# A linear recurrence layer on one core: x tiles spread unevenly over the level steps, tables requested sooner, narrower matmuls in the early levels of half 2

## The reference

```
h  = layernorm(x) * (1 + ca) + sa                # ca, sa, ga, ... from silu(c) @ wmod
per channel d:  s_t = A[d] s_{t-1} + Bm[d] h_t   # 16x16 matrix A[d], 8192 steps
                y_t = Cm[d] . s_t + Dm[d] h_t
x  = x + ga * (h + gelu(layernorm(y)*w + b) @ W_out.T + b_out)
h  = layernorm(x) * (1 + cb) + sb
x  = x + gb * (per-feature relu net of (h @ Win) @ Wout + bout)
```

## Time and profile before

| | |
|---|---|
| runs shown | 767.56, 768.90, 769.18 us; median 768.9 |
| profiled execution | 774.0 us; span of the core in it 772.2 us; mean granted TensorE clock 0.984 |
| PE busy | 710.3 us, 92% |
| DVE, POOL, ACT busy | 534.2, 483.1, 470.9 us (69, 63, 61%) |
| level steps of half 1 | 10.5 to 113 us |
| level steps of half 2 | 216.6 to about 276 us |
| output stage | 389 us to the end |

### The profile page before, as it was taken

One profiled execution on the slowest core, in us unless ns is written; L12 is line 12 of the kernel. 1 busy time (PEld: TensorE's weight loads), 2 busy tenths in 40 slices (PEclk: granted clock), 3 DMA queues, 4 the chain that ended last, 5 costly groups with the idle time before them and its releaser, 6 DMA issues.

```text
span 772.2 us, 24718 instructions
## 1 busy us (share of the span) xinstructions
PE 710.3 (92%) x10079; PEld 496.8 (64%) x10079; DVE 534.2 (69%) x1192; ACT 470.9 (61%) x1007; POOL 483.1 (63%) x684
## 2 busy tenths in 40 slices
PE   5777979899999988898879999999999999999997
PEld 4656667788799977887634555554555555455564
DVE  7765867854653367745734688888888788887776
ACT  1647677133322363234345788888888888888872
POOL 5654561753445615763188987789888888887710
PEclk9989999999999999999979999999999999999999
DMA  7967500139600000289342003322322332231114
GB/s 216 324 234 250 204 3 17 43 78 176 161 7 5 4 17 10 57 197 201 93 183 110 1 1 110 106 88 81 110 83 83 111 109 83 83 109 55 47 45 156
DMA packets 78257, 78.18 MB, mean 101 GB/s; under 512 B 16192, under 2 KB 49600, under 8 KB 78144
## 3 DMA queue, kind: packets, MB, share of 16 engines
q1 hardware_dynamic: 77120, 74.76, 31.9%
q10 hardware_dynamic: 1024, 1.84, 0.9%
HBM read 59.28 MB, written 17.30 MB: 99 GB/s over the span
## 4 chain that ended last, share of the span: by engine, by line
PE 49%; DVE 1%; POOL 0%; ACT 0%; DVEq 0%; issue 0%; ACTq 0%; POOLq 0%
PE PS L1304 30%; PE PS L1373 4%; PE PS L1351 4%; PE PS L1296 4%; PE PS L1338 4%; PE PS L1388 1%; PE PS L1314 1%; PE PS L1325 0%; ACT arenaC L660 0%; DVE ebs L975 0%; PE PS L1318 0%; DVE arenaC L991 0%; DVEq L81 0%; POOL sy L388 0%; DVE XY L829 0%
## 5 line engine op out<-in xcount | busy, mean ns | idle before, releaser
L1304 PE MATMUL PS<-arenaC,arenaA 128*128 128x512 f32 x512 | 242.2, 606 | 0.0
L404 POOL TENSOR_TENSOR arenaC<-arenaA,par 128x512 f32<-128x512 f32 x104 | 107.2, 1039 | 86.1 <-ACT arenaA L643 41.6
L1304 PEld LDWEIGHTS PS<-arenaC,arenaA 128*128 128x128 f32 x512 | 90.2, 191 | 87.8 <-issue 83.3
L1167 PE MATMUL PS<-arenaA,arenaC 64*64 64x80 f32 x1792 | 121.4, 236 | 18.6 <-DVE arenaC L817 13.5
L1170 PE MATMUL PS<-arenaA,arenaC 64*64 64x64 f32 x1792 | 118.7, 221 | 1.6 <-issue 1.6
L696 ACT ACTIVATE arenaA<-PS,ffc 128x256 f32<-128x256 f32 x224 | 111.7, 577 | 12.3 <-PE PS L1351 12.3
L1167 PEld LDWEIGHTS PS<-arenaA,arenaC 64*64 64x64 f32 x1792 | 94.1, 139 | 26.0 <-DVE arenaC L817 15.6
L1021 DVE SCALAR_TENSOR_TENSOR PS<-arenaA,ffc,PS 128x256 f32<-128x256 f32 x196 | 95.2, 486 | 22.3 <-ACT arenaA L696 5.7
L817 DVE STREAM_TRANSPOSE arenaC<-arenaC 128x512 f32<-128x512 f32 x104 | 72.6, 703 | 42.2 <-POOL arenaC L404 38.4
L1170 PEld LDWEIGHTS PS<-arenaA,arenaC 64*64 64x64 f32 x1792 | 98.6, 137 | 1.8 <-issue 1.8
L668 ACT ACTIVATE arenaA<-PS,lnwb 128x256 f32<-128x256 f32 x128 | 65.7, 574 | 44.5 <-PE PS L1296 44.5
(11 more groups left out here) (198 smaller groups left out, 1251.9 us busy)
## 6 DMA issues: line engine op xcount, KB each, us to landing
arenaC<-kernel_taps SPq DMA_DIRECT2D x64, 256.0 KB, 4.6
XY<-in_L_attn_x SPq DMA_DIRECT2D x38, 256.0 KB, 6.1
arenaC<-in_L_attn_x SPq DMA_DIRECT2D x15, 512.0 KB, 3.7
out<-arenaC SPq DMA_DIRECT2D x15, 512.0 KB, 2.7
arenaC<-in_L_attn_x SPq DMA_DIRECT2D x26, 256.0 KB, 4.8
XY<-in_L_wmod SPq DMA_DIRECT2D x6, 1024.0 KB, 9.0
XY<-in_L_attn_x SPq DMA_DIRECT2D x11, 512.0 KB, 3.6
out<-XY SPq DMA_DIRECT2D x10, 512.0 KB, 2.8
```

Source lines behind the costliest of these rows:

```text
L404: gp.tensor_tensor(BDs[:, step % BDR, :, :].rearrange("p g (a m) -> p g a m", m=NS), src, msk, ALU.mult).then_inc(S["bdp_r"], 1)
L1167: pe.matmul(pv_ps(r)[e:e + BW, j, 0:LW + NS], BDTs[e:e + BW, b, j, :], PV[e:e + BW, g, PW - LW:PW + NS], start=True, stop=True)
L1304: mm = pe.matmul(PS[:, 2 + t, :], zT[:, u % 2, q, t * P:(t + 1) * P], WoT[:, q, :], start=False, stop=(q == QB - 1))
```

## The change

Five edits: (1) `stats_of` and `tiles_of` follow two tables. The statistics are 2 tiles a step through step 25, with 5 more in step 12, 4 more in step 18 and one more in 13, 21 and 25; the normalisation is 2 tiles a step from step 3 on (it was from 4 on), with 2 and 3 more in steps 12 and 13, 2 more in 18 and 19 and one more in 20, 22, 24, 25 and 26. (2) The first four wmod tables are requested behind tiles 12, 15, 18 and 21 instead of 13, 17, 21 and 25. (3) The first half of A is loaded by one DMA instead of four. (4) In half 2, steps 0 to 19, the matmuls take 32 of the ready columns instead of 64: 48 and 32 columns instead of 80 and 64; the weight loads stay. (5) The waits on A's semaphore are adapted to (3).

```
-MOD_AT = (13, 17, 21, 25, 40, 44)
-STAT_STEPS, NORM_FIRST, NORM_STEPS = 25, 4, 23
+MOD_AT = (12, 15, 18, 21, 40, 44)
+STAT_SHARE = [2 if n < 26 else 0 for n in range(28)]
+NORM_SHARE = [2 if n >= 3 else 0 for n in range(28)]
+for step, more in ((12, 5), (13, 1), (18, 4), (21, 1), (25, 1)):
+    STAT_SHARE[step] += more
+for step, more in ((12, 2), (13, 3), (18, 2), (19, 2), (20, 1), (22, 1), (24, 1), (25, 1), (26, 1)):
+    NORM_SHARE[step] += more
...
             def load_A(half):
-                for o in range(OCT):
-                    load_A_part(half, o)
+                sp.dma_start(PV[:, :, PW:PW + NS], Av[:, half * HG:(half + 1) * HG, :]).then_inc(S["ld_A"], 16)
...
-                    gp.wait_ge(S["ld_A"], 16 * OCT * (half + 1))
+                    gp.wait_ge(S["ld_A"], 16 + 16 * OCT * half)
...
+                    nw = LW // 2 if half and n < 5 * OCT else LW
                     for j in range(8):
                         g = 8 * o + j
                         for e in QD:
-                            pe.matmul(pv_ps(r)[e:e + BW, j, 0:LW + NS], BDTs[e:e + BW, b, j, :], PV[e:e + BW, g, PW - LW:PW + NS],
+                            pe.matmul(pv_ps(r)[e:e + BW, j, LW - nw:LW + NS], BDTs[e:e + BW, b, j, :], PV[e:e + BW, g, PW - nw:PW + NS],
                                       start=True, stop=True)
                         for e in QD:
-                            mm = pe.matmul(w_ps(r)[e:e + BW, j, 0:LW], BDs[e:e + BW, b, j, :], WP[e:e + BW, g, L + 1 - LW:L + 1],
+                            mm = pe.matmul(w_ps(r)[e:e + BW, j, LW - nw:LW], BDs[e:e + BW, b, j, :], WP[e:e + BW, g, L + 1 - nw:L + 1],
```

More of the change, by code:

```diff
@@ L245, in stats_of @@
         def stats_of(n):
-            return range(min(NC * n // STAT_STEPS, NC), min(NC * (n + 1) // STAT_STEPS, NC))
+            return range(min(sum(STAT_SHARE[:n]), NC), min(sum(STAT_SHARE[:n + 1]), NC))
         def tiles_of(n):
-            return range(*(NC * min(max(m - NORM_FIRST, 0), NORM_STEPS) // NORM_STEPS for m in (n, n + 1)))
+            return range(min(sum(NORM_SHARE[:n]), NC), min(sum(NORM_SHARE[:n + 1]), NC))
         block = ctx.enter_context(nc.Block())
@@ L789, in first_column @@
             def first_column(half):
-                dve.wait_ge(S["ld_A"], 16 * OCT * (half + 1))
+                dve.wait_ge(S["ld_A"], 16 + 16 * OCT * half)
                 dve.wait_ge(S["mix_mm"], half + 1)
```

## The result

The changed kernel takes 762.8 us in the median of 6 runs (760.1 to 764.8), against 769.0 for the kernel before in the same comparison: a ratio of 0.9926, 95% interval 0.9901 to 0.9951. A second timing on the chip gave 0.9918 [0.9896, 0.9941]. So it is 6.3 us faster, where 14.5 us were forecast. The profiled execution of the changed kernel took 764.8 us, span 763.1, mean clock 0.983. Beside the 774.0 us of before that looks like 9.2 us; the 3 us between this and the medians turn out to matter.

A forecast was written before the change was run, and what follows sets the result against it. Half 1 was taken as bound by a loop of x-tile loads, normalisation and statistics, half 2's steps 0 to 19 by PE alone. From 768.9 us, 10.5 (half 1) and 4 (half 2) came off: 754.4 us, range 746 to 763.

The forecast's parts named there:

- the block at the loads' pace of 57 ns: Half 2, steps 0 to 19: four weight loads set a block at 0.229 us, a step at 1.83, saving 4 us.
- The rival in which columns alone count: Half 2: time follows streamed columns, not weight loads, 1.2 us a step, 16.6 us saved, 741.8 us in all; chance 0.06.
- The rival of the clock: Half 2: narrower matmuls let the clock fall to 1.2 GHz, 20 steps cost 29 us, 787 us in all; chance 0.04.
- This term of the sum: Half 1: new tile shares and sooner tables bring the taps 11.4 us sooner in an ideal replay, taken as 10.5 us.
- no DMA wait of DVE over 1 us before 45 us: Half 1, sign of being right: DVE's waits of 3.24 and 3.95 us for tiles 22 and 26 go.
- Within a microsecond of 63: Half 1, step 18: when the sixth table should land, behind tile 44, letting PE start the last two tables' products.
- The wait of PE over 3 us for the sixth table: Half 1, step 18: a sign that would show the forecast wrong; named for the fourth or sixth table.
- CM would hold the taps back for another 1 us: End of half 1: POOL fills CM after tile 63's normalisation, so taps start 1 us later than ACT allows, about 101.7.
- The 0.9 us by which 10.5 was taken under 11.4: Half 1: the replay gave taps 11.4 us sooner; 10.5 us was taken because every link in it is ideal.
- Tables sooner and the single DMA for A: Start of half 1: single DMA for A and tables behind 12, 15, 18 give nothing, or cost up to 1 us.
- the wait moves on: Rival, half 1: tables ahead of tile 22 and PE's stalls give back half, gain 5 us, 759.9 us; chance 0.20.
- half 1 gives nothing: Rival: ACT's normalisation is the real bound, so half 1 gains nothing, 764.9 us in all; chance 0.05.

The follow-up runs named there:

- after_again: The changed kernel with nothing edited, timed and profiled a second time: 0.9918 [0.9896, 0.9941] of the kernel before.
- after_third: The changed kernel with nothing edited, run for a third profile of its half 1; no separate time or ratio is given for it.
- cols24: The changed kernel with matmuls of 40 and 24 columns in steps 0 to 15 of half 2: 0.9940 [0.9918, 0.9961] of the kernel before.
- cols16: The changed kernel with matmuls of 32 and 16 columns in steps 0 to 15 of half 2: 1.0278 [1.0250, 1.0307] of the kernel before.
- norm_end: The changed kernel with the last two tiles' normalisation in step 26, ahead of its eviction, instead of step 27: 0.9905 [0.9886, 0.9924] of the kernel before.
- shares_only: The kernel before with only the new shares of x tiles per step in half 1 (edit 1): 0.9958 [0.9930, 0.9986], 3.2 us faster.
- narrow_all: norm_end with the blocks of 48 and 32 columns in half 1's steps 0 to 19 too: 1.0006 [0.9987, 1.0024] of the kernel before.

## Why the prediction was wrong

**Half 2 was right.** Forecast: the block at the loads' pace of 57 ns, 1.83 us a step, 4 us saved, at clock 1.00. Measured: 58 ns a load (0.233 us over four), 1.87 us a step, 3.3 us of the profile (40.72 to 37.45 between the same evictions) and 3.8 [2.0, 5.5] in the timing of this edit alone. Not every execution gives all of it: in after_again and after_third this stretch took 39.17 and 38.14 us, with short stalls of PE, at clock 1.00, that no execution with wide blocks has (40.72 in all of them). The rival in which columns alone count fell with cols24. (Its own terms give 1.25 us a step and 15.7 us saved, not the 1.2 and 16.6 of the prediction.) The rival of the clock did not happen at 48 and 32 columns, but its mechanism is real and came at 32 and 16: cols16 costs 21 us, and my reason against it, that the clock falls only behind an idle PE, was wrong.

**Half 1 was mis-sized: 10.5 us forecast, 3.4 measured.** This term of the sum is the step that failed. Its links, in absolute times, held up to 63 us: step 12's transposes at 41.0 (41.19), the table products near 42 (44.05, and 0.9 us shorter than the 4.57 taken), eviction 12 at 48.6 (49.92), no DMA wait of DVE over 1 us before 45 us (none from 15 us on), step 18's transposes at 63 (63.74). Three sizes were wrong; the means are over the executions in the table, without the first one of before:

- *The baseline, 4.2 us.* The forecast subtracted its replay from the times of one profiled execution, 774.0 us, and only in the last line carried the difference over to a median of 768.9, as if the 5.1 us between them lay outside half 1. Most of them lay in it: taps at 113.1, against 108.9 in the mean of the three other executions. What was replayed was an ideal execution, and what it was taken from a slow one.
- *The last table's products, 2.6 us.* "Within a microsecond of 63" was wrong: PE began them at 66.9 to 70.0 us in the six executions of the changed half 1. I had put the table behind the normalisation of tile 30 and given its transfer no time of its own, though a table sent at 68.08 had released its products only at 77.49. It was sent at 59.6, with the DMAs at 384 GB/s, and PE could go on at 69.2. The wait of PE over 3 us for the sixth table, named as a sign of error, came true in three of the six; in the others that wait was 1.8 us or less, behind DVE's waits for tiles and PE's "issue" stalls, and the products still began no sooner than 66.9. How much each of the three costs is open. Eviction 18 started at 75.5 in the mean, forecast 70.9 (its own terms, 63 + 5.32 + 2.04, give 70.4); 2.1 of these 4.6 us were caught up in steps 19 to 27. The last eviction ended at 103.1 (103.95 in the profile above, 1.33 behind its start), forecast 100.6. That CM would hold the taps back for another 1 us was right: 104.3, forecast 101.7.
- *What comes behind a wait, 0.9 us.* PE idles 2.2 to 3.0 us before the taps. In four of the six executions the clock then falls (0.66 over 105 to 110 us in the profile above), and from the taps to the scan it is 19.3 us in their mean instead of the 17.9 of before; in the other two it is 17.9. The forecast had nothing for this. norm_end shows both what the wait and what the clock cost: with CM in time the taps start 1.4 us after the last eviction's start, not 2.6, and the scan 17.9 us after the taps.

11.4 us at the taps, less 4.2, 2.6 and 0.9, leaves 3.7 at the scan, and so do the means of the table, 126.8 and 123.1. The timing has 3.4. The 0.9 us by which 10.5 was taken under 11.4 was the whole allowance for all three.

**The other small terms.** Tables sooner and the single DMA for A were put at nothing, and shares_only shows as much gain as all of half 1 without them; the single DMA was never run alone. The measured 762.8 us lies between two of the cases that were priced, "the wait moves on" at 759.9 us and "half 1 gives nothing" at 764.9, a little nearer the second. By its mechanism it is the first, for a reason that it half names: a wait moved, but from tile 22 to the tiles and the table of step 18, and PE's own stalls stayed.

The best version is the one with the last normalisation in step 26: 759.9 and 760.3 us, 0.9905 and 0.9908.

## What to carry to other kernels

Before a replay is subtracted from a profile, ask whether the profiled execution stands for the median, and in which stage it does not: 5 us of a forecast of 14.5 us were there to be seen in the times. Give every transfer that a step needs the time that such a transfer took in the trace, and where one stream brings all inputs, add up the bytes due by each step. And look for short waits of TensorE that a change makes, since the clock behind them can cost half as much again. Once matmuls are so narrow that a block takes the same time with fewer columns, still narrower ones gain nothing and can lose the clock.

## What the runs showed of the hardware that was not expected

- The granted clock can fall to 0.50 in an unbroken run of matmuls: blocks of 32 and 16 columns with loads of 64 columns did it in the third step, blocks of 40 and 24 did not in 16 steps.
- What the same blocks get depends on what the clock was before them: 48 and 32 columns kept 1.00 in half 2, but stayed at half for 12 steps in half 1 (narrow_all) and for four steps in half 2 (cols16), until wider matmuls came.
- The profile's clock reads 1.00 at the start of every trace where the blocks' pace is that of 1.2 GHz. In the kernel with narrow blocks in half 1 this went on to 55 us:

```profile
30.00:35.00 5.00, 5.00 (x98) 5.00 (x98) 3.97 (x10) 2.14 (x8) 2.66 (x5) 1.00 1.03 377
```

98 matmuls in 5 us is about 3.3 us for a step's 64, with a clock column of 1.00, where the same blocks at full clock take 1.87: at the start of a trace the pace is to be trusted, not the column.
